# Reordered seams of a two-block graph, attention and feed-forward kernel, and key sums on GpSimd

## The reference

```python
xn = _layernorm(x)
x = x + _L0_gnn_ref(xn, edge_index, edge_weight, W, b) + _L0_mix_ref(xn)  # q, k = elu + 1; z = 1 / (q . sum of k)
x = x + _L0_ffn_ref(_layernorm(x))       # 7 layers on nibbles; y with two one-hots added to columns 128 to 159
xn = _layernorm(x)
x = x + _L1_gnn_ref(xn) + _L1_mix_ref(xn)
    # gnn: relu(A @ ((xn @ U * s) @ Vt) + bias)
    # mix: q = softmax(q, axis=-1); k = softmax(elu(k) + 1.0, axis=-2)    (over the nodes)
    #      context = k.T @ v; out = (q @ context) @ w_proj + b_proj
x = x + _L1_ffn_ref(_layernorm(x))       # a gelu network on the low band of a Haar transform
```

## Time and profile before

| | us |
|---|---|
| median of three runs | 639.48 (638.75 to 640.98) |
| the profiled execution | 642.34 |
| its span, first to last instruction | 640.6 |
| TensorE busy in the span | 570.3 (89%) |
| VectorE | 478.9 (75%) |
| ScalarE | 328.4 (51%) |
| GpSimd | 259.0 (40%) |
| mean granted clock of TensorE | 0.968 |

### The profile page before, as it was taken

How to read it: one execution, slowest core, us unless ns; L and a number is a source line. 1 busy time by engine, 2 the same in 40 slices (tenths; PEclk the granted TensorE clock), 3 DMA queues, 4 the chain that set the end, 5 groups by cost and what they waited for, 6 DMA issues and landing times.

```text
span 640.6 us, 8669 instructions
## 1 busy us (share of the span) xinstructions
PE 570.3 (89%) x2939; PEld 460.1 (72%) x2939; DVE 478.9 (75%) x1044; ACT 328.4 (51%) x619; POOL 259.0 (40%) x290
## 2 busy tenths in 40 slices
PE   3988899989999798999999939998979997998976
PEld 2767787667778586888776627777867886686866
DVE  7689998979996777578968766666765555677764
ACT  7867886767656612122147534445346774323161
POOL 4747776756787215346716920004010221022020
PEclk9999999999999898999999969998999997999979
DMA  9300000000010201113040200000020000110004
GB/s 316 123 2 1 1 1 2 2 1 1 2 67 2 65 0 34 34 36 74 13 140 3 65 0 1 1 0 2 0 83 0 1 1 1 36 49 0 1 4 158
DMA packets 15045, 21.11 MB, mean 33 GB/s; under 512 B 3260, under 2 KB 6000, under 8 KB 15002
## 3 DMA queue, kind: packets, MB, share of 16 engines
q1 hardware_dynamic: 13674, 17.94, 8.9%
q10 hardware_dynamic: 1328, 2.62, 1.2%
HBM read 18.00 MB, written 2.56 MB: 32 GB/s over the span
## 4 chain that ended last, share of the span: by engine, by line
PE 58%; DVE 21%; ACT 6%; issue 6%; POOL 4%; DMA 3%; DVEq 1%; SPq 1%; ACTq 0%; POOLq 0%
PE p L2050 6%; PE p L1887 4%; PE p L2168 4%; PE pQ L2168 4%; PE pQ L1903 3%; PE pH L1903 3%; DVE onehot L1294 3%; PE p L2285 2%; PE p L2135 2%; PE pKV L2135 2%; PE pQ L2347 2%; PE pH L2062 2%; PE p L1903 1%; PE pKV L1932 1%; DMA nodes<-in_x 1%
## 5 line engine op out<-in xcount | busy, mean ns | idle before, releaser
L973 POOL TENSOR_TENSOR Loh<-onehot,whl 128x512 fp32r<-128x512 f32 x85 | 89.4, 1052 | 47.7 <-DVE onehot L1294 47.7
L1294 DVE TENSOR_SCALAR onehot<-iota_src,srclo 128x128 fp32r<-128x128 f32 x170 | 74.8, 480 | 0.7 <-DVE flagint L1306 0.7
L2050 PE MATMUL p<-G,ATs 128*128 128x512 f32 x300 | 73.5, 402 | 0.0
L1887 PEld LDWEIGHTS p<-Roh,Loh 128*128 128x128 f32 x340 | 47.6, 190 | 31.6 <-issue 27.7
L2050 PEld LDWEIGHTS p<-G,ATs 128*128 128x128 f32 x300 | 57.7, 194 | 12.7 <-issue 0.7
L1887 PE MATMUL p<-Roh,Loh 128*128 128x200 f32 x340 | 53.2, 279 | 11.8 <-POOL Loh L973 4.6
L564 ACT ACTIVATE away<-iota_key,key 128x200 f32<-128x200 f32 x85 | 38.8, 456 | 24.3 <-PE p L1887 24.2
L1903 PE MATMUL pQ<-wsl,xT 128*128 128x512 f32 x168 | 47.4, 411 | 2.4 <-DVE xT L1208 2.4
L1903 PE MATMUL pH<-wsl,xT 128*128 128x512 f32 x168 | 45.4, 397 | 0.0
L1145 POOL TENSOR_TENSOR xT<-xn,xT 128x512 fp32r<-128x512 f32 x10 | 12.9, 1288 | 74.7 <-ACT xT L795 74.3
L991 POOL TENSOR_TENSOR ATs<-AT,ATs 128x1280 fp32r<-128x1280 f32 x10 | 29.5, 2950 | 29.7 <-ACT ATs L624 29.4
(11 more groups left out here) (629 smaller groups left out, 1448.8 us busy)
## 6 DMA issues: line engine op xcount, KB each, us to landing
xb<-in_x SPq DMA_DIRECT2D x9, 256.0 KB, 2.7
out<-nodes SPq DMA_DIRECT2D x9, 256.0 KB
wraw<-in_L_mix_w_qkv ACTq DMA_DIRECT2D x2, 1024.0 KB, 7.8
raw<-in_L_mix_w_qkv SPq DMA_DIRECT2D x2, 1024.0 KB, 5.1
nodes<-in_x SPq DMA_DIRECT2D x1, 1024.0 KB, 9.1
wraw<-in_L_mix_w_qkv SPq DMA_DIRECT2D x1, 1024.0 KB, 11.4
wraw<-in_L_gnn_W SPq DMA_DIRECT2D x1, 1024.0 KB, 13.6
raw<-in_L_mix_w_out SPq DMA_DIRECT2D x1, 1024.0 KB, 5.2
```

What stands on the lines that cost most here:

```text
L973: pool.tensor_tensor(Loh[:, g % SLOTS], o, w, ALU.mult).then_inc(S["oh_pool"], 1)
L1294: ins = v.tensor_scalar(onehot_[:, g % SLOTS, c, :], iota_src[:], srclo[:, 2 * g + c:2 * g + c + 1], None, ALU.is_equal)
L1887: ins = pe.matmul(pW[g % 2][:, 0:T * WIN], Loh[:, g % SLOTS, c, part, :], Roh[:, g % RSLOTS, c, :], start=(c + part == 0), stop=(c + part ...
L2050: ins = pe.matmul(pG[u][:, :], ATs[:, u, x, s_, :], G[:, y, s_, :], start=(s_ + n == 0), stop=(s_ == T - 1 and n == 2))
```

## The change

It moves work on all four engines' lists in the six places above, and computes the key sums of the second block elsewhere.

- First block: folded weights ahead of the last queries, in the order 0, 1, 3, 2, with their evictions; key sums go to bank `pA` and `q_scaled` reads them there, with a copy to SBUF at tile 5 for tile 9; turns of scaled queries 0 and 1 behind pieces 7 and 9; GpSimd's bias additions wait for `qs_ok` 1; `aggregated(0)` ahead of the low part of tile 1.
- Network: layers 20 to 23 ahead of the first turn, 24 behind it, evictions interleaved with `answers` (now in two parts, with their results in PSUM banks `rbank`) and with the norm coefficients (statistics and root apart).
- Second block: for the second group the statistics come at tile 3 and the root at tile 4; `norm1` ahead of `ln_sqrt(6)`; the loop ends at tile 7; the last turn lies inside the key product of tile 8; the queries of tiles 8 and 9 come behind the key product of tile 9.
- Keys: no products with ones. GpSimd adds up exp of the keys in `ksums` (`z_sum`), and ahead of `keys(9)` four fp32 products of two columns turn the sums over partitions. The scalings follow `keys(9)` directly, four adjacency steps come later, `kT` ahead of the last four evictions.

```diff
-    act.wait_ge(S["ksb_ps"], 1)
-    act.activation(xn[:, 0, :], pH[:, :], ACT.Copy).then_inc(S["ksb_ok"], 1)
+    def m_hi(p):
+        act.wait_ge(S["m_mm"], MORDER.index(p) + 1)
+        act.activation(WO[:, 0, p, :], mbank[p][:, :], ACT.Copy).then_inc(S["m_hi"], 1)
+
+    m_hi(0)
+    m_hi(1)
...
+    m_hi(3)
...
         if t == T // 2:
             q_out(T - 1, et, pT)
+            m_hi(2)
         act.activation(G[:, 0, t, :], nodes[:, t, :], ACT.Copy, scale=dinv[:, t:t + 1]).then_inc(S["g_hi"], 1)
     qt_hi(0)
-    for p, bank in enumerate(mbank):
-        act.wait_ge(S["m_mm"], p + 1)
-        act.activation(WO[:, 0, p, :], bank[:, :], ACT.Copy).then_inc(S["m_hi"], 1)
...
+    relu(20)
+    relu(21)
     ln_sqrt(5, *GROUPS[0])
-    relu(20)
+    relu(22)
...
     norm1(0, 0, True)
-    relu(21)
     xt1_hi(0, 0)
+    relu(23)
     norm1(1, 1, True)
-    relu(22)
-    relu(23)
...
+        for k in BESIDE_Q[t]:
+            relu(k)
+        xt1_hi(t + 1, (t + 1) % 2)
+        first_exp(t)
+        for k in BESIDE_TURN[t]:
+            relu(k)
+        first_elu(t)
         for k in BESIDE_K[t]:
...
+        norm1(t + 2, t % 2)
         if t == 3:
             ln_sqrt(6, *GROUPS[1])
-        if t + 2 < T:
-            norm1(t + 2, u)
+    xt1_hi(T - 1, (T - 1) % 2)
+    first_elu(T - 2)
+    first_ulow(T - 2)
+    first_elu(T - 1)
...
+            act.wait_ge(S["z_one"], t - 1 + after["z_one"])
...
+    first_ulow(T - 1)
     a2_hi(0)
     a2_hi(1)
     act.wait_ge(S["cmb_ps"], 1 + after["cmb_ps"])
     act.activation(kmaxb[:], pH[:, :], ACT.Copy).then_inc(S["cmb_ok"], 1)
     zexp(0, 0, True)
+    first_exp(T - 2)
+    a2_hi(2)
     zexp(1, 1, True)
-    a2_hi(2)
     a2_hi(3)
+    first_exp(T - 1)
...
+        if t == T - 1:
+            act.wait_ge(S["zr_ok"], 1 + after["zr_ok"])
+            act.wait_ge(S["z_mm"], T + after["z_mm"])
+            for b, bank in enumerate((pK, pV)):
+                act.activation(xn[:, b, :], bank[:, :], ACT.Copy, scale=ksum[:, b:b + 1]).then_inc(S["zs_a"], 1)
...
+    pool.wait_ge(S["qs_ok"], 1)
...
+    pool.wait_ge(S["ln_ok"], 6)
...
+    def z_sum(t):
+        rows = LAST if t == T - 1 else P
+        pool.wait_ge(S["z_exp"], t + 1 + after["z_exp"])
+        e = (et, rt)[t % 2][0:rows, :]
+        if t == 0:
+            pool.wait_ge(S["nq_exp"], T - 1 + after["nq_exp"])
+            ins = pool.tensor_copy(ksums, e)
+        else:
+            pool.wait_ge(S["z_one"], t + after["z_one"])
+            ins = pool.tensor_tensor(ksums[0:rows, :], ksums[0:rows, :], e, ALU.add)
+        ins.then_inc(S["z_one"], 1)
+
     z_xlo(0, 0)
     pool.wait_ge(S["u_lo"], T)
     z_xlo(1, 1)
+    z_sum(0)
+    z_sum(1)
     for t in range(2, T):
         z_xlo(t, t % 2)
+        z_sum(t)
...
+        if t == T - 1:
+            v.wait_ge(S["ksb_ok"], 1)
+        if t == 5:
+            v.tensor_copy(xn[:, 0, :], pA[:, :]).then_inc(S["ksb_ok"], 1)
+        step(v.tensor_tensor(et[:], qv, pA[:, :] if t < T - 1 else xn[:, 0, :], ALU.mult))
...
+    m_lo(3)
...
+    for t in range(5):
+        g_lo(t)
+    q_elu(T - 1, et, pT)
+    v.wait_ge(S["q_elu"], T)
+    m_lo(2)
+    for t in range(5, 8):
+        g_lo(t)
+    v.wait_ge(S["ksb_ps"], 1)
+    q_scaled(0)
+    g_lo(8)
+    g_lo(9)
...
+        rs = rbank[g][:, 64:64 + 2 * n].rearrange("p (t q) -> p t q", q=2)
...
+            step(v.tensor_copy(first[:, :, pos].rearrange("p (c u) -> p c u", u=2), r6[:, :, pos, :, 0]))
+            step(v.tensor_tensor(rs[:, :, pos].rearrange("p (c u) -> p c u", u=2), first[:, :, pos].rearrange("p (c u) -> p c u", u=2),
+                                 r6[:, :, pos, :, 1], ALU.add))
...
+        h = rbank[g][:, 128:128 + 32 * n].rearrange("p (t j) -> p t j", j=32)
...
+        ln_variance(t0, t1)
+
+    def new_roots(g):
+        t0, t1 = GROUPS[g]
+        ln_roots(5 + g, t0, t1, rbank[g][:, 96:96 + t1 - t0])
...
     rest_of(19)
+    answered(0)
+    rest_of(20)
     new_coefficients(0)
-    rest_of(20)
+    rest_of(21)
+    new_roots(0)
+    rest_of(22)
     xt1_lo(0, 0)
-    rest_of(21)
-    rest_of(22)
     rest_of(23)
+    rest_of(24)
...
+        first_sub(t)
...
+        xt1_lo(t + 1, (t + 1) % 2)
...
         if t == 2:
             answers(1)
+            answered(1)
         if t == 3:
             new_coefficients(1)
+        if t == 4:
+            new_roots(1)
+        first_elu(t)
+        first_sum(t)
+        for k in BESIDE_K[t]:
+            rest_of(k)
+        first_u(t)
+    xt1_lo(T - 1, (T - 1) % 2)
+    first_elu(T - 2)
+    first_u(T - 2)
+    first_elu(T - 1)
...
-    step(v.tensor_reduce(ksum[:], pQ[:, :].rearrange("p (c n) -> p c n", c=KC), AX, ALU.max))
-    for p in range(PAIRS):
-        ins = v.tensor_scalar(et[:, p * P:(p + 1) * P], onesf[:], ksum[:, p:p + 1], None, ALU.mult)
-    ins.then_inc(S["cm_ok"], 1)
+    step(v.tensor_reduce(ksum[:], pKV[0][:, :].rearrange("p (c n) -> p c n", c=KC), AX, ALU.max))
+    v.tensor_tensor(et[:].rearrange("p (c n) -> p c n", c=KC), onesf[:].rearrange("p (c n) -> p c n", c=1).broadcast_to([P, KC, P]),
+                    ksum[:].rearrange("p (c n) -> p c n", n=1).broadcast_to([P, KC, P]), ALU.mult).then_inc(S["cm_ok"], 1)
+    first_sub(T - 2)
+    first_u(T - 1)
...
     a2_lo(0)
-    a2_lo(1)
     v.wait_ge(S["cmb_ok"], 1 + after["cmb_ok"])
     z_sub(0)
+    a2_lo(1)
+    first_sub(T - 1)
+    z_lo(0, 0)
     z_sub(1)
-    z_lo(0, 0)
     z_lo(1, 1)
     a2_lo(2)
     a2_lo(3)
-    v.wait_ge(S["sq"], 2 * T)
-    step(v.reciprocal(sumq[:], sumq[:]))
...
+    def column_sums():
+        v.wait_ge(S["zc_ps"], 1 + after["zc_ps"])
+        v.wait_ge(S["z_klo"], T + after["z_klo"])
+        v.reciprocal(ksum[:], pKV[0][:, 0:2 * PAIRS].rearrange("p (b n) -> p b n", n=2)[:, :, 0]).then_inc(S["zr_ok"], 1)
+        v.wait_ge(S["zr_ok"], 1 + after["zr_ok"])
+        v.wait_ge(S["z_mm"], T + after["z_mm"])
+        for b, (bank, o) in enumerate(((pH, et), (pQ, rt))):
+            v.tensor_scalar(o[:], bank[:, :], ksum[:, 2 + b:3 + b], None, ALU.mult).then_inc(S["zs_d"], 1)
+
...
+        if t == 1:
+            first_sum(T - 2)
+            first_sum(T - 1)
+        if t == 2:
+            v.wait_ge(S["sq"], 2 * T)
+            step(v.reciprocal(sumq[:], sumq[:]))
+        if t == T - 1:
+            column_sums()
...
-    v.wait_ge(S["z_one"], T + after["z_one"])
-    v.wait_ge(S["z_klo"], T + after["z_klo"])
-    diag = et[:].rearrange("p (c n) -> p c n", c=KC)
-    step(v.tensor_tensor(diag, pKV[0][:, :].rearrange("p (c n) -> p c n", c=KC),
-                         ident[:].rearrange("p (c n) -> p c n", c=1).broadcast_to([P, KC, P]), ALU.mult))
-    step(v.tensor_reduce(ksum[:], diag, AX, ALU.add))
-    v.reciprocal(ksum[:], ksum[:]).then_inc(S["zr_ok"], 1)
-    v.wait_ge(S["zr_ok"], 1 + after["zr_ok"])
-    v.wait_ge(S["z_mm"], T + after["z_mm"])
-    for b, (bank, o) in enumerate(((pH, et), (pQ, rt))):
-        v.tensor_scalar(o[:], bank[:, :], ksum[:, 2 + b:3 + b], None, ALU.mult).then_inc(S["zs_d"], 1)
-    a2_lo(24)
-    a2_lo(25)
...
+    folded(0)
+    pe.wait_ge(S["dhl_lo"], 1)
+    degrees(0, 4)
+    folded(1)
+    degrees(4, 7)
+    folded(3)
+    degrees(7, T)
+    pe.wait_ge(S["xt_lo"], T)
+    for c in range(KC):
+        for n, (x, y) in enumerate(THREE):
+            ins = pe.matmul(pT[:, :], xT[:, (T - 1) % XR, x, c, :], wsl[:, WQ, y, c, :], start=(c + n == 0), stop=(c == KC - 1 and n == 2))
+    ins.then_inc(S["q_mm"], 1)
+    pe.wait_ge(S["q_elu"], T - 1)
+    folded(2)
+    pe.wait_ge(S["bd_ok"], 1)
+    pe.wait_ge(S["deg_ok"], 1)
     for p in range(PAIRS):
-        ins = pe.matmul(pH[:, p * P:(p + 1) * P], bdk[:, p * P:(p + 1) * P], ident[:], start=True, stop=True)
+        ins = pe.matmul(pA[:, p * P:(p + 1) * P], bdk[:, p * P:(p + 1) * P], ident[:], start=True, stop=True)
     ins.then_inc(S["ksb_ps"], 1)
...
-    last_q(0, 2)
...
-        if s_ == 2:
+        if s_ == 7:
             q_transposes(0)
-        if s_ == T - 2:
-            q_transposes(1)
+    q_transposes(1)
     mix(0)
     mix(1)
     q_transposes(2)
...
+            pe.wait_ge(S["qs_ok"], T - 1)
...
-    layer(20)
+    for k in range(20, 24):
+        layer(k)
     turn(0, 0, True)
-    for k in range(21, 24):
-        layer(k)
-    for t in range(T):
+    layer(24)
...
+    first_u(T - 2)
+    first_k(T - 1)
+    first_q(T - 2)
...
+        pe.matmul(sbank[0:RANK, 0:n * P], uhl[:, s_, 0:RANK], ATr[:, (k + 2) % RING, 1, 0:n * P], start=False, stop=(s_ == T - 1),
                   skip_group_check=True).then_inc(S["a2_mm"], 1)
-    pe.wait_ge(S["n_lo"], T + after["n_lo"])
+    pe.wait_ge(S["kmax_ok"], T)
+    for c in range(KC):
+        ins = pe.transpose(pKV[0][:, c * P:(c + 1) * P], kmax[:, c * P:(c + 1) * P], ident[:])
+    ins.then_inc(S["cm_ps"], 1)
+    first_u(T - 1)
     turn_weights(0)
     turn_weights(1)
-    pe.wait_ge(S["kmax_ok"], T)
-    for c in range(KC):
```

(17 more changed lines are left out.)

205 lines of the change are left out of this document (100 added, 105 removed).

## The result

The changed kernel takes 612.76 us (median of 4, 609.15 to 613.66), the kernel before 640.21 us in the same runs (638.75 to 640.98): a ratio of 0.956, 95% interval 0.952 to 0.961. The forecast was 603.3 us with a range up to 610.0. The sign and most of the steps were right, but the gain is 27.4 us and not 36.2, and the time lies 2.8 us above the range. One execution among the later ones, of the kernel before, took 721.91 us at a mean granted clock of 0.745; it is left out of every figure here.

What follows compares the result with a forecast made beforehand. TensorE, the fullest engine, was taken to bound the kernel, losing time at seams to holes and the lowered clock behind them. Gains of 9.6 + 9.0 + 5.0 + 5.3 + 3.2 + 4.1 = 36.2 us took 639.5 to 603.3 us, range 598.8 to 610.

Steps and rivals of the forecast that it cites:

- The basis: Whole kernel: gains taken in a profiled execution of 642.34 us were carried unchanged to the median of 639.48 us.
- (f): Behind the keys loop: scalings start at once, the 2.98 us hole becomes 0.5, Z turns at full clock; gain 4.1 us.
- the clock takes part of it back: Rival: new holes of 0.5 to 1.3 us standing close together lower TensorE's clock again; 609 us, chance 0.17.
- (b): Seam into the second block: layers reordered around the first turn, answers kept in PSUM; gain 9.0 us.
- (d): Between second-block loop and keys loop: two query products move behind the last key product into holes; gain 5.3 us.
- 1.58 us alone didn't: Argument against the clock's fall: behind a 1.58 us hole, the next twelve products still took 3.01 us.
- (e): Keys loop: twenty products with ones go, GpSimd sums and four small products replace them; gain 3.2 us.
- no cost: Keys loop: GpSimd's sums, at 2.6 of 4.57 us a tile, were to delay nothing, being needed two tiles later.
- the rival's mechanism: Rival for the keys loop: GpSimd's sums hold VectorE, tiles take 4.8 us instead of 4.57; 606.8 us, chance 0.10.
- (c): Second block's loop: holes of 1.58 and 1.99 us and the slow product behind them go; gain 5.0 us.
- (a): Seam behind the first block's last product: work reordered, key sums read from PSUM, two holes shrink or go; gain 9.6 us.
- all upper ends: Rival: everything hides, so every part of the change reaches its highest gain; 599 us, chance 0.09.

Runs made afterwards that it cites:

- the second profile: The changed kernel run again with no edit, to see its scatter and its clock behind the keys loop: 610.85 us, ratio 0.955.
- the second profile of the kernel before: The kernel before run again with no edit, to see its scatter: 642.49 us median of nine executions, the profiled one 643.87 us.

## Why the prediction missed, step by step

**The basis (2.9 us of 9.5).** "What lies around the span stays, so a difference in the span is carried over to the median unchanged": the time around the span did stay (1.74 us in both), but the span that the sum started from was not that of a median execution. Single executions of the kernel before have a standard deviation of 2.1 us (55 of them), so a gain read from one profile has an error of some 2 us on either side before any step is wrong, and the range contained nothing for it.

**(f), 0.0 instead of 4.1: the largest miss.** The order worked as told: the hole went from 2.98 to 0.75 us, and the turn of Z ran at full clock, in 1.8 us. The failed step is the term behind it, "Behind it 39 products remain in 4.57 us after VectorE's low parts, as now: 7.7 us". From the turn of Z to the end of the products with Wv it took 10.3 us, because the clock was at 1.2 GHz from 512.0 us on; with the clock up, in the second profile, the same took 7.8. The forecast treated the low clock as part of the long hole, to vanish with it. It did not vanish but came later and stayed longer: before, it was low for some 7 us, mostly under the 16 transposes and the two steps behind them, now for some 10 us, under the products with Wv and the adjacency steps. The next term was too small as well: the last steps, put at 3.5 us, take 5.1, and 4.4 with the clock up, for waits of 0.81, 0.24 and 0.19 us on VectorE. With the clock up the stretch gains 3.3 us, so 0.8 us of the forecast were too much and 3.3 are the clock.

This is the rival "the clock takes part of it back", put at 0.17 and 609 us; its mechanism decided, in (f) alone and not in (b) and (d), where no fall followed holes of 0.3 to 1.1 us. What brings the clock down here, the three waits or the narrow work, is supported for the waits and not proven. What spoke against the rival ("1.58 us alone didn't") came again in the second profile of the kernel before; it was a single wait among products of 512 columns, and says nothing of three waits among narrower ones.

**(e), 1.8 instead of 3.2.** The tile time was right (4.55 against 4.57), and the small products too (0.92 us). Two terms were too small. The wait for the last sum was put at 0.3 and is 0.54, since the addition takes 1.73 us beside VectorE and not 1.29. The start of the loop was put at 0.7 (in (d)) for the first tile, and then 1.13 us are waited ahead of the second. There the step "no cost" failed: the sums stand beside VectorE's subtraction and low part, which took 1.10 and 1.22 us, and 0.68 and 0.69 with the sums taken out. The row that spoke against it, a 0.70 us subtraction, started 0.15 us before the end of a GpSimd one; it could not have shown a wait of more than that, so it was no evidence. In the steady loop the rival's mechanism is there and costs nothing: the subtraction of the maximum takes 1.78 us instead of 0.68 in the last five of its ten instructions, but the low part, which TensorE waits for, takes 0.70.

The Trainium skill gives this rule on the page SBUF — State Buffer, section Who interferes with whom: a VectorE instruction with two SBUF inputs contends with a GpSimd instruction that reads SBUF, and one waits for the whole of the other, while one with at most one SBUF input outside the two-port modes doesn't contend. It counts copies, casts and `tensor_scalar`, the instruction of the clamps, among those that can enter a two-port mode. The rows agree: 1.78 against 0.68 us with two SBUF inputs, 2.84 against 0.18 for a clamp moved from PSUM to SBUF, and 0.68 for the adjacency's low parts with one input in PSUM, beside a GpSimd instruction in the same loop. They go beyond it in one thing: the clamp waited not for the one instruction at work but for the rest of the queue.

**(c), 3.5 instead of 5.0.** The two holes and the slow product went, as told. In their place came three waits of 0.47, 0.46 and 0.45 us. The first is GpSimd: "Wv copies ... lie in an engine idle for tens of us" priced the engine and not its neighbour, and a cast and a subtraction of VectorE took 2.4 us instead of 0.4. The two others wait for ScalarE's second reading of bank `pK`, with no query product between two key products any more; one had been priced (0.35 us, in (d)), the other forgotten.

**(a), (b), (d): right.** 9.9, 9.9 and 5.9 us against 9.6, 9.0 and 5.3. The first query product starts 13.08 us behind layer 20 (356.88 to 369.96), forecast 13.1; the hole of tile 1 is 1.34 us, forecast 1.2; the clamp takes 0.18, forecast 0.17; no clock was lost at any of the three. That the operands' place and not only the order did it is shown by the run with SBUF operands. In (d) the keys loop's first tile waited 0.40 us where 0.7 was put; the wait ahead of the second tile, which falls into (e), is the other side of it.

**Not foreseen:** 1.2 us at the start, which is scatter: the first folded product starts at 203.9 to 206.0 us in the twelve profiles of changed kernels, the key sums of the kernel before at 203.94 and 205.15.

**Its sums.** They hold within 0.1 us, with three exceptions that change nothing in the verdict on the steps: the lower end of (a) is 6.6 us by its own terms and not 6, all upper ends together are 41.7 us and give 597.8 us and not 599, and the stretch of (f) is 19.2 us long in the profile before, up to the transposes at 552.30, and not 18.7.

## What to carry to other kernels

Before a gain is added up from a profile, see where that execution stands among the others, and put the scatter into the range. Price an engine that is idle by its neighbours too: work that GpSimd does in SBUF is paid by VectorE's instructions with operands there, so put it where VectorE waits anyway, or give VectorE its operand in PSUM, even for twelve columns. A seam is worth its hole plus the clock behind it, and a seam with several short waits can lose as much clock as one with a long one, in some executions and not in others. If nothing useful fits, unread products in an unused bank are worth a try: behind the keys loop the clock held in three of three profiles with them. They have to start when the wait starts and end before it does, and the gain has to be looked for in the times, not only in the stretch.

## What was not expected of the hardware

- The granted clock fell to 0.50 behind waits of 0.54, 0.75 and 0.49 us within 9.5 us, 3.5 us after the last of them had ended, while TensorE was busy with 128-column products; in another execution of the same kernel it didn't. Behind the 1.34 us wait among 512-column products it fell in none of eleven profiles; behind the wait of 1.99 us of the kernel before, twelve such products took 4.58 and 4.59 us in its two profiles.
- Executions of one program on one chip differ by up to 9 us in 640 (635.6 to 645.0); 1.4 us between its two profiles were there at 100 us already.
- A clamp of 12 columns waited 2.7 us for a whole run of GpSimd subtractions to end, although one of them takes 1.25 us and the next ones had not begun when it was due.
